# Expert layers as plain fp32 products from unsplit weights, seven whole-row gathers in flight, and a new order for the last tile

## The chip, the cores and the metric

The kernel runs on one core of one Trainium2 chip. The metric is the device time of one execution, in microseconds (us); lower is better. 0.3% of it, 2.4 us, is about what a measurement of this kernel can tell from no change.

## What is computed

Three residual blocks over x, 32 batches of 32 tokens with 512 features (1024 tokens):

```
x = x + cross_attention(layernorm(x), ctx, ctx, mask)      # 16 heads, 257 keys per batch
x = x + self_attention(layernorm(x))                       # 16 heads, rms-normed q and k
x = x + ffn(layernorm(x))

def ffn(x):
    x_mixed = k0 * x[s-1] + k1 * x[s] + k2 * x[s+1]        # along the tokens of a batch
    scores  = tanh(x_mixed @ Wo1 + bo1) @ Wo2 + bo2        # 9 scores for each token
    p       = argmax(scores)                               # one expert of 9
    y       = (x_mixed @ W1[p] + b1[p]) @ W2[p] + b2[p]    # 512 -> 128 -> 512, no nonlinearity
    return layernorm(x + y) * gamma + beta
```

The reference computes all nine experts and picks one; the kernel computes only the chosen one.

## The kernel before, in words

The kernel is written engine by engine, with semaphores and an order written out by hand. `T` is 1024 tokens, `P` is 128, so there are `NT` = 8 token tiles; `D` is 512, `CT` = 4 is the number of 128-wide chunks of a row, `E` is 9.

Cross attention comes first and is not touched, apart from where its weight tile `W_both` is allocated. Most products of both attentions are made as three products of split operands: every fp32 operand is cut into a high part, rounded to the reduced format `fp32r`, and the rest, and `three` (L92 to L96) issues high by high, low by high, high by low. `W_both` holds the high and low parts of five weights.

Self attention (`self_attention_and_experts`, L769) goes over the eight tiles in a software pipeline: iteration `it` projects q, k, v of tile `it - 1`, computes scores of tile `it - 2` and the output projection of tile `it - 3`. The last iterations are written out by hand, and with them the first part of the experts:

- `z3_make` writes the third layernorm of a tile, `z3_transposes` turns it, `mix_parts` (ScalarE) and `mix` (GpSimd) make the mixed rows, transposed, in `O_T`. For the last tile `mix_end` shares this between ScalarE, VectorE and GpSimd.
- `gate`, `tanh`, `gate_scores`, `choose` pick an expert for each token, in four groups of tiles (0 to 3, 4 and 5, 6, 7).
- `positions` (TensorE), `find_places` and `mark_places` (VectorE) and `map_tile` (TensorE, one tile at a time through the two buffers of `placed`) sort tokens by expert. `census`, `ranks`, `slot_lists` and `list_tokens` turn that into `NS` = 16 slots of up to 128 tokens of one expert, with the lists `to_slot` (which rows to fetch) and `from_slot` (where results go).
- `rows_transposes` and `rows_evac` turn the mixed rows back, and SyncE stores them to the DRAM tensor `rows`, whose rows hold 3 x 512 values: mixed row, `z3` row, and `x` plus `beta`. `m_rows` also stores the mixed rows alone in `rows_first`.
- The expert weights come in six loads of 768 KB into the two halves of `raw` and are split into `W_both`, as its attention weights fall out of use: `w_split` on ScalarE (L1698, one instruction a load) and on VectorE (L1976, three a load).

Then the sixteen slots run through all engines. GpSimd issues the gathers. Slots 0 and 1 fetch their mixed rows from `rows_first` into `z2` and `k_T` (`gather_first`), then whole rows (768 KB a slot) are fetched into a ring of seven buffers, `gather(k)`. Five are issued at once; slot 5 waits for the last weight split, and the rest go out one a slot:

```
for k in range(NS):
    make_root(k)
    if k:
        scatter(k - 1)
    if k + RING - 2 < NS:
        gather(k + RING - 2)
```

TensorE's order in the loop is `h_transpose(k - 1)`, `x_transposes(k + 1)`, `hidden(k)`, `outputs(k - 1)`. ScalarE's is `h_high(k - 1)`, `x_high(k + 1)`, `h_evac(k)`, `deviations(k - 2)`. VectorE makes the low parts (`x_low`, `h_low`) and does `residual`, `centre`, `finish`. `make_root(k)` on GpSimd needs the sum of squares of `deviations(k)`; `scatter(k)` writes 256 KB of finished rows to the output.

`idle` (L1477) issues products whose result nobody reads.

Of the kernel before, what the change touches and what calls it, by code (L numbers as in the profile page):

```python
# [60 lines left out]
def build(nc, io, out):  # L61
    ctx = ExitStack()
    with ctx:
# [14 lines left out]
        W_both = sb("W_both", [P, 2, 5, CT * D], F32R)  # L78
        W_hi, W_lo = W_both[:, 0], W_both[:, 1]
# [8 lines left out]
        cross_attention(nc, io, x_nat, ident, O_T, raw, W_hi, W_lo, bv, bo, o_b, o_first, w_in, whi, wlo, seen)  # L88
        self_attention_and_experts(nc, io, out, x_nat, ident, O_T, raw, W_both, bv, bo, o_b, first_pair, w_in, whi, wlo, seen)
# [678 lines left out]
def self_attention_and_experts(nc, io, out, x_nat, ident, O_T, raw, W_both, bv, bo, o_b, first_pair, w_in, whi, wlo, seen):  # L768
# [7 lines left out]
    with ExitStack() as ctx:  # L776
# [12 lines left out]
        e_both = W_both[:, :, :, :].rearrange("p a i n -> p a (i n)")  # L789
        w_hi, w_lo = ([W[:, i, :].rearrange("p (c n) -> p c n", c=CT) for i in range(5)] for W in (W_hi, W_lo))  # L790
        e_hi, e_lo = (W[:, :, :].rearrange("p i n -> p (i n)") for W in (W_hi, W_lo))
# [47 lines left out]
        GROUPS = ((0, 4), (4, 6), (6, 7), (7, 8))  # L839
        wo2, bo1, bo2 = sb("wo2", [P, E]), sb("bo1", [P, 1]), sb("bo2", [P, E])  # L840
# [10 lines left out]
        place, of_block = sb("place", [P, NT]), sb("of_block", [P, NT])  # L851
        place_i = sb("place_i", [P, NT], I32)
        placed = sb("placed", [P, 2, P + NB])
        junk9 = sb("junk9", [P, E])
# [9 lines left out]
        def th_of(g):  # L864
            at = (0, 0, 2 * P, 3 * P)[g]
            return bqkv[:, 1, at:at + (GROUPS[g][1] - GROUPS[g][0]) * P]

# [6 lines left out]
        rows_first = nc.dram_tensor("rows_first", (T, D), F32).ap()  # L874
# [5 lines left out]

        first_rows = (z2[:, :], k_T[:, :, :].rearrange("p c t -> p (c t)"))
# [10 lines left out]
        def x_halves(k):  # L892
            return (o_hi, o_lo) if k % 2 == 0 else o_first

        def h_rows(k):
            return z3s[:, k % 2 * 2 * P:(k % 2 + 1) * 2 * P]

        def h_halves(k):
            return z2_hi[:, k % 2, :], z2_lo[:, k % 2, :]


        def split_parts(i):

            src, n = raw[:, i % 2, 0:3 * D], 3 * D
            dst = [W[:, i * n:(i + 1) * n] for W in (e_hi, e_lo)]
            if i >= 3:
                return (src, *dst)
            return (src.rearrange("p (c e m) -> p c e m", c=CT, e=3),
                    *(w.rearrange("p (e c m) -> p c e m", c=CT, e=3) for w in dst))


        lists = (pw[0], pt[0], pw[0], pt[0])
        found = pw[0]
# [5 lines left out]
        def rows_bank(u):  # L919
            return pa[:, u % 2, :] if u else pw[1][:, :]  # L920
# [4 lines left out]
        def h_bank(k):  # L925
            return (pw[0][:, 0:2 * P], pa[:, 0, 0:2 * P])[k % 2]
# [4 lines left out]
        def y_bank(k):  # L931
# [4 lines left out]
        (w_hi_made, w_lo_made, mix_made, g_done, th_made, gs_done, choice_made, step3, pos_done, placed_made, map_done,  # L936
         counted, found_pe, found_dve, rowsT_done, rows_out) = (
            sem("x_" + n) for n in (
                "w_hi_made w_lo_made mix_made g_done th_made gs_done choice_made step3 pos_done placed_made map_done "
                "counted found_pe found_dve rowsT_done rows_out").split())  # L940
        (xT_done, xhi_made, xlo_made, h_done, h_out, hT_done, hhi_made, hlo_made, y_done, mean_made, squares_made,
         root_made, fin, last_mixed) = (
            sem("s_" + n) for n in (
                "xT_done xhi_made xlo_made h_done h_out hT_done hhi_made hlo_made y_done mean_made squares_made "
                "root_made fin last_mixed").split())
        x_first = [sem(f"x_first{i}") for i in range(2)]
# [40 lines left out]
        def _(eng):  # L987
# [1236 lines left out]
```

## Time and profile before

| | |
|---|---|
| median of 3 runs | 803.71 us (803.34 to 805.87) |
| the profiled execution, its own time | 801.18 us |
| its span, first to last instruction | 799.5 us |
| TensorE busy | 734.1 us (92%) |
| VectorE, ScalarE, GpSimd busy | 399.6, 345.4, 205.1 us |
| mean granted TensorE clock | 0.95 of full speed |
| HBM read, written | 47.45 MB, 12.58 MB |

The profile is of one execution. Its busy shares are an average over stages. The attentions take about the first 640 us, and there TensorE stands still little. The last 160 us look different: TensorE's share falls to 5 to 8 tenths, its granted clock falls with it, and the DMA engines are busy for 3 to 5 tenths. The change lies in these last 160 us, so it is read by stretches of time, by the timelines of TensorE and GpSimd there, and by the chain of waits.

### The profile page before, as it was taken

Reading aid. Unit: us, or ns where it says so; the run is one execution under the profiler, and the core shown is the slowest. Engines: PE = TensorE matmul, PEld = TensorE weight load, DVE = VectorE, ACT = ScalarE, POOL = GpSimd, SP = SyncE. Lnnn points to the kernel's source line nnn. Section 1 sums busy time; section 2 is a strip of 40 time slices with the busy share of each in tenths; the row PEclk is TensorE's granted clock in tenths of the full one; section 3 lists DMA queues with packets and bytes.
Section 4 is the critical chain, followed back from the end, with each engine's and each line's share of the span. In section 5 each row is a group of like instructions: output and inputs, shape, how many; then the busy total and the mean of one; then the engine's idle time right before and its main releaser. Section 6 shows DMA issues by size and latency. Waiting matters only on the chain. (4 is left out here: it accounts for less than half of the span.)

```text
span 799.5 us, 20785 instructions
## 1 busy us (share of the span) xinstructions
PE 734.1 (92%) x8232; PEld 582.1 (73%) x8232; DVE 399.6 (50%) x1045; ACT 345.4 (43%) x733; POOL 205.1 (26%) x299
## 2 busy tenths in 40 slices
PE   4999999999999999999999999899998986877773
PEld 3777778777877887787778777678777775666652
DVE  5544434343443244343424456657777767334555
ACT  3445444444444354444444454335445743222332
POOL 0001000010010010000100202776687642314455
PEclk9999999999999999999999999999999978577787
DMA  8211111011011101110120124300001135544540
GB/s 325 66 53 55 53 55 30 25 52 52 0 52 52 52 0 52 52 34 19 52 52 2 51 104 121 96 15 15 27 27 43 54 121 211 179 176 147 161 169 25
DMA packets 18871, 58.61 MB, mean 73 GB/s; under 512 B 6258, under 2 KB 6514, under 8 KB 15878
## 3 DMA queue, kind: packets, MB, share of 16 engines
q1 hardware_dynamic: 15078, 42.74, 15.8%
q0 software_dynamic: 3744, 15.21, 5.4%
q8 instruction: 32, 0.52, 0.3%
q14 instruction: 17, 0.14, 0.1%
HBM read 47.45 MB, written 12.58 MB: 75 GB/s over the span
## 5 line engine op out<-in xcount | busy, mean ns | idle before, releaser
L94 PE MATMUL pj<-W_both 128*128 128x512 f32 x544 | 222.4, 409 | 10.1 <-DVE W_both L593 10.1
L96 PE MATMUL pj<-W_both 128*128 128x512 f32 x544 | 213.8, 393 | 0.0
L95 PE MATMUL pj<-W_both 128*128 128x512 f32 x544 | 213.0, 392 | 0.0
L94 PEld LDWEIGHTS pj<-W_both 128*128 128x128 f32 x544 | 102.8, 189 | 43.8 <-issue 24.0
L96 PEld LDWEIGHTS pj<-W_both 128*128 128x128 f32 x544 | 102.8, 189 | 23.0
L95 PEld LDWEIGHTS pj<-W_both 128*128 128x128 f32 x544 | 103.1, 190 | 19.2
L234 POOL COPY q_b<-Q_T 128x128 f32 (+1 forms) x32 | 9.3, 292 | 416.9 <-PE tp L357 349.2
L491 ACT ACTIVATE K<-pj,bk 128x512 f32<-128x512 f32 x64 | 44.2, 690 | 136.9 <-PE pj L96 136.9
L652 DVE CUSTOM_DVE_ANT_0 m_flat<-sc,mask 128x257 f32<-128x257 f32 x64 | 24.7, 424 | 116.2 <-PE tp L357 94.9
L506 ACT ACTIVATE p_flat<-m_flat,nmax 128x257 f32<-128x257 f32 x128 | 63.8, 501 | 25.5 <-DVE nmax L652 25.4
L498 ACT ACTIVATE V<-pj 128x512 f32<-128x512 f32 x64 | 38.2, 597 | 73.1 <-PE pj L96 72.3
L593 DVE TENSOR_TENSOR W_both<-raw,W_both 128x2048 fp32r<-128x2048 f32 (+1 forms) x20 | 43.7, 2185 | 30.8 <-ACT W_both L450 30.8
L673 DVE COPY P_T<-tp 128x512 f32<-128x512 f32 x32 | 22.1, 691 | 66.6 <-PE tp L369 66.6
L1092 POOL TENSOR_TENSOR rms<-ms_eps,power 128x16 f32<-128x16 f32 x16 | 46.9, 2931 | 3.3 <-POOL ms_eps L1089 3.3
L661 DVE TENSOR_SCALAR p_flat<-p_flat,rinv 128x257 f32<-128x257 f32 x128 | 42.0, 391 | 1.1
L94 PE MATMUL pw<-W_both,z_hi 128*128 128x512 f32 x92 | 38.0, 413 | 1.0 <-DVE z_lo L1948 1.0
L450 ACT ACTIVATE W_both<-raw 128x2048 fp32r<-128x2048 f32 (+1 forms) x20 | 36.4, 1821 | 2.6 <-DMA raw<-wk_dram 2.6
L95 PE MATMUL pw<-W_both,z_lo 128*128 128x512 f32 x92 | 36.6, 397 | 0.0
L96 PE MATMUL pw<-W_both,z_hi 128*128 128x512 f32 x92 | 36.3, 395 | 0.0
L369 PE MATMUL tp<-ident,p_flat 128*128 128x128 f32 x256 | 33.1, 272 | 0.7 <-DVE P_T L673 0.7
L369 PEld LDWEIGHTS tp<-ident,p_flat 128*128 128x128 f32 x256 | 29.8, 140 | 4.8 <-issue 0.8
L684 DVE TENSOR_TENSOR O_T<-po,otail 128x128 f32 (+1 forms) x16 | 4.7, 292 | 43.4 <-PE po L389 43.3
(359 smaller groups left out, 1261.4 us busy)
## 6 DMA issues: line engine op xcount, KB each, us to landing
raw<-ctx_dram SPq DMA_DIRECT2D x15, 1024.0 KB, 4.7
raw<-w_dram SPq DMA_DIRECT2D x6, 768.0 KB, 4.5
raw<-w_dram SPq DMA_DIRECT2D x4, 1024.0 KB, 4.8
x_nat<-x_dram SPq DMA_DIRECT2D x2, 1024.0 KB, 12.5
rows<-z3s SPq DMA_DIRECT2D x8, 256.0 KB, 2.0
rows<-x_nat SPq DMA_DIRECT2D x8, 256.0 KB, 2.2
rows_first<-xm SPq DMA_DIRECT2D x8, 256.0 KB, 2.2
rows<-xm SPq DMA_DIRECT2D x8, 256.0 KB, 2.4
```

Of the source, the lines that this page charges most:

```text
L94: eng.matmul(out, a_hi, b_hi, start=first, stop=False)
L95: eng.matmul(out, a_lo, b_hi, start=False, stop=False)
L96: return eng.matmul(out, a_hi, b_lo, start=False, stop=last)
L369: mm = eng.transpose(tp[:, k, g * P:(g + 1) * P], probs[:, j, g, k * P:(k + 1) * P], ident[:, :])
L450: return eng.activation(dst, src, ACT.Copy)
L491: eng.activation(K[:, g, :, 0:SM], pj[g % 2][:, :].rearrange("p (j n) -> p j n", j=2), ACT.Identity, bias=bk[:, g:g + 1]).then_inc(k_out, 1)
L498: eng.activation(V[:, t, :], pj[t % 2][:, :], ACT.Copy).then_inc(v_out, 1)
L506: eng.activation(probs[:, j, g, :], masked[:, j, g, :], ACT.Exp, bias=nmax[:, j, g:g + 1], scale=-1.0, accum_out=psum_[:, j, g:g + 1]).the ...
L593: return eng.tensor_tensor(dst, src, hi.bitcast(F32), ALU.subtract)
L652: eng.tensor_tensor_reduce(masked[:, j, g, :], sc[g][:, 0:SK], mask[:, :], -1.0, BIG, ALU.add, ALU.min, nmax[:, j, g:g + 1]).then_inc(mask ...
L661: eng.tensor_scalar(probs[:, j, g, :], probs[:, j, g, :], rinv[:, j, g:g + 1], None, ALU.mult).then_inc(probs_made, 1)
L1092: eng.tensor_tensor(rms[:, heads], ms_eps[:, heads], power[:, heads], ALU.pow).then_inc(rms_made[i], 1)
```

## The change

It has four parts.

1. **Weights.** `experts`, plain fp32, takes the memory of `W_both` once a part of that is free. Layer one is in its first half (`w1_all`), layer two in its second (`w2_all`). SyncE loads straight into it, twelve DMAs: for layer one nine of 256 KB in pieces of 128 values, for layer two three of 768 KB. All `w_split` are gone, and with them gather 5's wait for the last split.
2. **Products.** `hidden` is a bias product and four fp32 products of 128 x 128, `outputs` a bias product and one fp32 product of 128 x 512; `h_transpose` is one transpose. ScalarE makes one copy where it made a high part (`xT_evac`, `hT_evac`), and `x_low`, `h_low` on VectorE are gone.
3. **Gathers.** `rows_first` and its eight stores are gone, as are `gather_first` and its two fetches. Seven gathers of whole rows are issued at once, then gather `k + 6` behind `scatter(k - 1)`.
4. **The last tile's order.** `map_tile` becomes `map_tiles` over three groups (`PLACED`: tiles 0 to 3, 4 and 5, 6 and 7), with marks for whole groups, `row_marks` and `block_marks`; `find_places` works on a group at once. `weighted_sum(NT + 1)` stands ahead of `gate_scores(1)`, `positions(0)` and the first `rows_transposes`; the four `idle` products between the last steps are gone, and the ten after them are four fp32 products.

```
-        W_both = sb("W_both", [P, 2, 5, CT * D], F32R)
+        with ExitStack() as attention:
+            W_both = sb("W_both", [P, 2, 5, CT * D], F32R, attention)
...
+        experts = sb("experts", [P, 2, 5, CT * D])
...
             def load(i):
-                need(eng, w_lo_made, 3 * (i - 1))
-                eng.dma_start(raw[:, i % 2, 0:3 * D], io["w1" if i < 3 else "w2"][i % 3]).then_inc(exw_in, 16)
-                eng.wait_ge(exw_in, 16 * (i + 1))
+                n = 3 * D
+                for j in range(3):
+                    eng.dma_start(w1_all[:, i * n + j * D:i * n + (j + 1) * D].rearrange("p (c m) -> p c m", c=CT),
+                                  io["w1"][i].rearrange("p (c e m) -> p c e m", c=CT, e=3)[:, :, j, :]).then_inc(exw_in, 16)
+                eng.dma_start(w2_all[:, i * n:(i + 1) * n], io["w2"][i]).then_inc(exw_in, 16)
...
             def m_rows(u):
                 eng.wait_ge(rows_out, u + 1)
-                eng.dma_start(rows_first[u * P:(u + 1) * P, :], mixed_rows(u)).then_inc(rows_in, 16)
                 eng.dma_start(at_rows(u, 0), mixed_rows(u)).then_inc(rows_in, 16)
...
             def gather(k):
-                if k < RING:
-                    if k == 5:
-                        eng.wait_ge(w_lo_made, 3 * 6)
-                else:
-                    eng.wait_ge(fin, k - RING + 1)
+                need(eng, fin, k - RING + 1)
...
-            for k in range(2):
-                gather_first(k)
-            for k in range(RING - 2):
+            for k in range(RING):
                 gather(k)
             for k in range(NS):
                 make_root(k)
                 if k:
                     scatter(k - 1)
-                if k + RING - 2 < NS:
-                    gather(k + RING - 2)
+                    if k + RING - 1 < NS:
+                        gather(k + RING - 1)
...
             def hidden(k):
-                out = h_bank(k).rearrange("p (i t) -> p i t", i=2)
                 for c in range(CT):
-                    for x in x_halves(k):
-                        eng.matmul(out, x[:, c, :], e_both[:, :, bass.ds(w_at + c * P, P)],
-                                   start=c == 0 and x is x_halves(k)[0], stop=False)
+                    mm = eng.matmul(h_bank(k), x_T(k)[:, c * P:(c + 1) * P], w1_all[:, bass.ds(w_at + c * P, P)],
+                                    start=False, stop=c == CT - 1)
...
             def outputs(k, w_at):
-                three(eng, y_bank(k), *h_halves(k), e_hi[:, w], e_lo[:, w], False, True).then_inc(y_done, 1)
+                eng.matmul(y_bank(k), h_T(k), w2_all[:, bass.ds(w_at, D)], start=False, stop=True).then_inc(y_done, 1)
```

**TensorE, one slot of the expert loop, before** (the end of slot 15's first layer, then slot 14's second; `first_pair` is the split rows, `z_hi` and `z_lo` the split hidden values, `z3s` the unsplit ones):

```order
L1504 MATMUL pa<-W_both,first_pair 128x256 x2
L1504 ISA
L1504 MATMUL pa<-W_both,first_pair 128x256 x2
L1506 MATMUL pa<-biases,of_slot 128x128
L1522 MATMUL pa<-biases,of_slot 128x512
L94 ISA
L94 MATMUL pa<-W_both,z_hi 128x512
L95 MATMUL pa<-W_both,z_lo 128x512
L96 ISA
L96 MATMUL pa<-W_both,z_hi 128x512
L1513 MATMUL pa<-ident,z3s 128x128 x2
```

and now, where the bias product of the first layer stands just ahead of these rows:

```order
L1476 ISA
L1476 MATMUL pa<-experts,e_T 128x128
L1476 ISA
L1476 MATMUL pa<-experts,e_T 128x128
L1476 ISA
L1476 MATMUL pa<-experts,e_T 128x128
L1476 ISA
L1476 MATMUL pa<-experts,e_T 128x128
L1489 MATMUL pa<-biases,of_slot 128x512
L1490 ISA
L1490 MATMUL pa<-experts,z3s 128x512
L1484 MATMUL pa<-ident,z3s 128x128
```

Eight products over 256 columns for each slot become four over 128, three over 512 become one, and two products that turn the hidden values become one transpose.

**TensorE, from the last tile's output projection to the lists, before** (`pa<-placed` is `map_tile`, `pa<-ident,O_T` is `rows_transposes`, `pa<-W_both` alone is `idle`):

```order
L1441 MATMUL pa<-placed 72x128
L1432 MATMUL pt<-choice,above 128x9
L1433 MATMUL pt<-chosen,ones 128x9
L1441 MATMUL pa<-placed 72x128
L1459 MATMUL pw<-ones,in_all 72x1
L1477 MATMUL pa<-W_both 128x512 x2
L1464 MATMUL pw<-used,above 72x1
L1477 MATMUL pa<-W_both 128x512 x2
L1441 MATMUL pa<-placed 72x128
L1470 MATMUL pw<-listed,tokens_T 128x16
```

and now:

```order
L1423 MATMUL pa<-sq_v,qk_qT 72x128 x2
L1412 MATMUL pw<-choice,above 128x18
L1413 MATMUL pw<-chosen,ones 128x18
L1439 MATMUL pw<-ones,in_all 72x1
L1433 MATMUL pa<-ident,O_T 128x128 x4
L1444 MATMUL pw<-used,above 72x1
L1433 MATMUL pa<-ident,O_T 128x128 x4
L1423 MATMUL pa<-sq_v,qk_qT 72x128 x2
L1450 MATMUL pw<-listed,tokens_T 128x16
```

The last two turns of rows stand where the idle products stood, and one group of two map products ends the list instead of single ones.

**GpSimd, the gathers, before:**

```order
L1198 DMA z<-rows_first,to_slot 128x512
L1198 DMA k_T<-rows_first,to_slot 128x512
L1207 DMA sq_v<-rows,to_slot 128x1536
L1207 DMA qk_qT<-rows,to_slot 128x1536
L1207 DMA xm<-rows,to_slot 128x1536
L1207 DMA O_T<-rows,to_slot 128x1536 x2
L1213 TENSOR_SCALAR root_in<-squares 128x1
L1214 TENSOR_TENSOR root<-root_in,power 128x1
L1207 DMA raw<-rows,to_slot 128x1536
```

and now:

```order
L1189 DMA sq_v<-rows,to_slot 128x1536
L1189 DMA qk_qT<-rows,to_slot 128x1536
L1189 DMA xm<-rows,to_slot 128x1536
L1189 DMA O_T<-rows,to_slot 128x1536 x2
L1189 DMA raw<-rows,to_slot 128x1536 x2
L1195 TENSOR_SCALAR root_in<-squares 128x1
L1196 TENSOR_TENSOR root<-root_in,power 128x1
L1195 TENSOR_SCALAR root_in<-squares 128x1
L1196 TENSOR_TENSOR root<-root_in,power 128x1
L1202 DMA out_dram<-xm,from_slot 1024x512
L1189 DMA sq_v<-rows,to_slot 128x1536
```

Gathers of slots 5 and 6 moved from behind the first roots to the opening burst; slot 7's is the first that a root holds back, root 1.

## Rows read from the trace of the kernel before

**Rows 1.** Stretches of 20 us: busy us (instructions) by engine, clock, DMA share, GB/s.

```profile
660.00:680.00 20.00, 13.51 (x77) 11.80 (x78) 13.71 (x45) 6.64 (x15) 3.92 (x7) 0.84 0.57 213
680.00:700.00 20.00, 16.40 (x66) 12.62 (x64) 7.06 (x27) 4.53 (x8) 7.00 (x7) 0.61 0.53 186
...
740.00:760.00 20.00, 15.79 (x70) 12.44 (x70) 10.97 (x24) 6.05 (x16) 8.87 (x13) 0.76 0.50 160
760.00:780.00 20.00, 15.10 (x76) 11.55 (x76) 11.13 (x26) 7.29 (x20) 10.56 (x15) 0.90 0.43 162
```

**Rows 2.** TensorE's timeline, last tile and first slots: start us, us, line, operation, count [idle before].

```profile
660.41 0.77 PE L94 MATMUL pw<-W_both,o_hi 128*128 128x512 f32 x1 [1.53 <-issue]
...
672.65 0.38 PE L1357 MATMUL pw<-ident,z3s 128*128 128x128 f32 x2
...
677.44 0.44 PE L1441 MATMUL pa<-placed 128*72 128x128 f32 x2 [3.83 <-DVE placed L2040]
...
686.86 1.20 PE L1477 MATMUL pa<-W_both 128*128 128x512 f32 x2
...
689.54 0.32 PE L1472 MATMUL pw<-listed,expert_of 72*41 72x16 f32 x2
...
694.67 1.12 PE L1488 MATMUL pt<-ident,z 128*128 128x128 f32 x4 [0.24 <-DMA z<-rows_first,to_slot]
...
703.67 1.11 PE L1488 MATMUL pt<-ident,xm 128*128 128x128 f32 x4 [3.65 <-DMA xm<-rows,to_slot]
```

**Rows 3.** GpSimd's timeline: first gathers, one slot's work late in the loop, last scatter.

```profile
691.01 1.35 POOL L1198 DMA_INDIRECT z<-rows_first,to_slot  x1 [13.71 <-DVE from_slot L2074]
...
766.51 0.42 POOL L1213 TENSOR_SCALAR root_in<-squares 128x1 f32<-128x1 f32 x1 [1.61 <-ACT e L1740]
...
769.19 1.00 POOL L1207 DMA_INDIRECT sq_v<-rows,to_slot  x1 [0.30 <-issue]
...
794.08 0.99 POOL L1220 DMA_INDIRECT out_dram<-xm,from_slot  x1 [0.30 <-issue]
```

**Rows 4.** Chain that ended last, one turn in the expert loop: start us, us, what.

```profile
768.69 0.67 PE pt L1488 x4
...
771.33 0.81 ACT e L1740 x2
...
774.65 4.58 DMA qk_qT<-rows,to_slot
779.27 0.66 PE pt L1488 x4
```

**Rows 5.** TensorE's timeline: two fp32 product groups (L1411), then one expert slot.

```profile
641.47 1.88 PE L1411 MATMUL pw<-O_T,raw 128*128 128x512 f32 x4
...
668.55 1.16 PE L1411 MATMUL pw<-O_T,raw 128*128 128x128 f32 x8 [1.74 <-DVE placed L2040]
...
774.88 1.21 PE L1504 MATMUL pa<-W_both,first_pair 128*128 x8 [0.23 <-issue]
...
776.18 0.44 PE L1522 MATMUL pa<-biases,of_slot 41*128 41x512 f32 x1
776.55 0.50 PE L94 MATMUL pa<-W_both,z_hi 128*128 x1
...
777.37 0.61 PE L1513 MATMUL pa<-ident,z3s 128*128 128x128 f32 x4
```

**Rows 6.** The same columns as rows 1, four us in the opening burst of gathers.

```profile
700.00:704.00 4.00, 0.35 (x3) 0.34 (x3) 0.29 (x1) 0.28 (x1) 0.00 (x0) 0.82 1.00 393
```

**Rows 7.** Instructions that touch `rows` from 685 us on: their DMA time.

```profile
DMA to landing us min/median/max: 4.6/5.3/8.5
```

**Rows 8.** Groups by line from 620 us on: count, busy us, mean ns, idle before.

```profile
L1976 DVE TENSOR_TENSOR W_both<-raw,W_both 128x512 fp32r<-128x512 f32 x18 | 11.3, 679 | 0.0
L1698 ACT ACTIVATE W_both<-raw 128x1536 fp32r<-128x1536 f32 x6 | 9.0, 1494 | 1.7 <-DMA raw<-w_dram 1.7
```

**Rows 9.** The page's DMA queue of SyncE: packets, MB, share of 16 engines.

```profile
q1 hardware_dynamic: 15078, 42.74, 15.8%
```

More of the change, by code:

```diff
@@ L890, in result, with x_T, h_T @@
             return xm[:, 1, k % 3 * D:(k % 3 + 1) * D]
-        def x_halves(k):
-            return (o_hi, o_lo) if k % 2 == 0 else o_first
+        def x_T(k):
+            return (e, e_T)[k % 2]
         def h_rows(k):
[L896 to L909, printed above, removed]
+            return z3s[:, k % 2 * P:(k % 2 + 1) * P]
+        def h_T(k):
+            return z3s[:, (2 + k % 2) * P:(3 + k % 2) * P]
         lists = (pw[0], pt[0], pw[0], pt[0])
+        places = (pw[0], pt[0], pw[0])
         found = pw[0]
@@ L1031, in _ @@
                     x_rows(u - 1)
+            eng.wait_ge(wo_done, NT)
+            load(0)
+            z_rows(5)
+            eng.wait_ge(qkv_done, 3 * NT - 2)
+            load(1)
+            eng.wait_ge(qkv_done, 3 * NT - 1)
             load(2)
[L1033 to L1034 removed]
             x_rows(4)
             x_rows(5)
[L1037 removed]
+            eng.wait_ge(x1b_made, NT)
+            eng.dma_start(gamma, row_on_all(io["gamma"])).then_inc(exw_in, 16)
             z_rows(6)
+            m_rows(0)
+            z_rows(7)
+            for u in range(1, 5):
+                m_rows(u)
             x_rows(6)
[L1040 to L1048 removed]
             x_rows(7)
[L1050 to L1051 removed]
+            for u in range(5, NT):
+                m_rows(u)
         @block.gpsimd
@@ L1424, in gate_scores, with positions @@
                 mm.then_inc(gs_done, 1)
-            def positions(g):
-                a, b = GROUPS[g]
-                to = lists[g][:, 0:(b - a) * E]
-                eng.wait_ge(choice_made, g + 1)
-                need(eng, counted, b - 1)
+            def positions(q):
+                a, b = PLACED[q]
+                to = places[q][:, 0:(b - a) * E]
+                eng.wait_ge(choice_made, q + 1 if q < 2 else len(GROUPS))
+                eng.wait_ge(counted, b - 1)
                 eng.matmul(to, above[:, :], choice[:, a:b, :].rearrange("p t e -> p (t e)"), start=True, stop=False)
@@ L1655, in mix_parts @@
                 eng.wait_ge(mix_made, u + 1)
-                for a, dst in ((1, O_T), (0, o_b), (2, mixed)):
+                for a in some:
+                    dst = (o_b, O_T, mixed)[a]
                     for c in range(CT):
@@ L1739, in deviations @@
                 need(eng, squares_made, k)
-                eng.activation(e[:, :], slot(k, 1), ACT.Square, bias=mean[:, k:k + 1],
+                eng.activation(mixed[:, :, :].rearrange("p c t -> p (c t)"), slot(k, 1), ACT.Square, bias=mean[:, k:k + 1],
                                accum_out=squares[:, k:k + 1]).then_inc(squares_made, 1)
@@ L1795, in _ @@
                     deviations(k - 2)
-            h_high(NS - 1)
+            hT_evac(NS - 1)
             deviations(NS - 2)
@@ L2021, in choose, with find_places @@
                                              in1=before, op0=ALU.is_equal, op1=ALU.add).then_inc(counted, 1)
-            def find_places(g):
-                a, b = GROUPS[g]
-                eng.wait_ge(choice_made, g + 1)
-                eng.wait_ge(pos_done, g + 1)
-                for t in range(a, b):
-                    ch3.link(eng.tensor_tensor_reduce(junk9[:, :], lists[g][:, (t - a) * E:(t - a + 1) * E], choice[:, t, :], 1.0, 0.0,
-                                                      ALU.mult, ALU.add, place[:, t:t + 1]))
+            def find_places(q):
+                a, b = PLACED[q]
+                n = b - a
+                got = places[q][:, 0:n * E].rearrange("p (t e) -> p t e", t=n)
+                eng.wait_ge(choice_made, q + 1 if q < 2 else len(GROUPS))
+                eng.wait_ge(pos_done, q + 1)
+                eng.wait_ge(counted, b)
+                ch3.link(eng.tensor_tensor(key[:, 0:n, :], got, choice[:, a:b, :], ALU.mult))
+                eng.tensor_reduce(place[:, a:b], key[:, 0:n, :], AX.X, ALU.add).then_inc(places_made, 1)
+                eng.wait_ge(places_made, q + 1)
                 ch3.link(eng.tensor_copy(place_i[:, a:b], place[:, a:b]))
```

304 lines of the change are left out of this document (102 added, 202 removed).

## The prediction

> **What bounds the kernel now.** I read the stretches of time first, then TensorE's timeline, the chain of waits, and GpSimd's timeline. Up to 640 us TensorE is nearly always busy, and the change leaves that part alone. From 660 us on it is busy for 13.5 to 16.4 us of every 20, at a granted clock between 0.61 and 0.90 of full speed [rows 1]. Two stages lie there. Up to the lists of rows to fetch, ready at 689.9 us, TensorE hands small results to VectorE and waits for them, once for 3.83 us [rows 2]. Then come the sixteen slots: first gather at 691.0 us, last scatter at 794.1 us, end of the span at 799.5 us [rows 3]. So the expert loop is 108.5 us.
>
> In the loop no engine is full. The chain of waits shows a ring: the turn of slot 13's rows at 768.69, the deviations at 771.33, the gather at 774.65 with 4.58 us to landing, the turn of slot 15's rows at 779.27 [rows 4]. That is 10.6 us for two slots, 5.3 a slot, with the clock up; it is longer where the clock is down. The gather of slot k + 5 goes out behind root k. Root k needs `deviations(k)`, which ScalarE has behind `h_evac(k + 2)`, and that needs slot k + 3's rows, which TensorE turns ahead of `hidden(k + 2)`. So a gather is issued only two slots ahead of its use, though the ring of buffers has seven places. Latency sets the pace.
>
> **The loop, step by step.** *Lead.* Now gather k + 6 stands behind root k, three slots ahead. The same chain, 10.6 us, spread over three slots, is 3.5 us a slot.
>
> *GpSimd* then comes first. Root, scatter and gather of one slot run from 766.51 to 770.19 us [rows 3]: 3.7 us, with the hand-over 3.8 us. Nothing of it is removed. I take 3.8.
>
> *TensorE.* A slot at full clock now: turn of rows 0.45 (four transposes, shown as 0.67 with the tail [rows 4]), first layer with bias 1.30, second 1.19, turn of hidden values 0.5 (spacing of the starts, and the last row's 0.61 less its tail [rows 5]); with hand-overs 3.9. After the change: an fp32 product over 512 columns takes 0.9 us (1.88 us for two), one over 128 takes 0.25 to 0.29 (1.16 us for four, less the tail) [rows 5]. So first layer 1.0 + 0.15 for the bias, second 0.35 + 0.9, one transpose 0.11, rows 0.45: 2.9 us. At half clock it is some 5.7 us. Even here TensorE gains 1.0 us a slot, and its gaps, 0.9 us in 3.8, are shorter than those of the stretch whose clock was 0.90 [rows 1].
>
> The first layer gains although the array's work stays the same. In the old form eight products took 1.21 us [rows 5]. The Trainium skill, "FP8 and Floating Point Precision", section "TensorE Precision Notes", says that true FP32 takes four passes through the array. By it alone the first layer is 4 x 128 x 4 columns against 8 x 256, no gain, and the second 512 x 4 against 3 x 512, a loss of 512 columns, 0.2 us at full clock; the sum would then owe nothing to the products. The 0.9 us for 512 columns agrees with four passes, so I book only the 1.0 us above, most of it from the turn of the hidden values and the first layer's shorter issue.
>
> *VectorE* loses the two low parts of each slot and *ScalarE* has the same count of copies; both have room below 3.8 us, so I book nothing but their part in the tail.
>
> *Start.* The opening gathers run at 393 GB/s with the DMA engines full [rows 6]; a gather of 786,432 B then takes 2.0 us, and 5.3 us from issue to landing [rows 7]. Slot 0's rows are there 5.4 us after the first issue; before, the small fetch let TensorE start after 3.7 (694.67 less 691.01) [rows 2, 3]. That is 1.7 us lost. But slot 2 lands at 9.4 where five big gathers behind two small ones had it at 12.7 (the turn at 703.67, after a wait of 3.65 us [rows 2]), and slot 6 at 17.6. Counting from the first issue: first layer of slot 0 ends at 10.0, each slot takes 2.9, slot 3's first layer ends at 18.0, so root 1 can start at 19.2, and gather 7 starts 2.7 later, at 21.9 (766.51 to 769.19 in rows 3). Eight more gathers at 3.8 put gather 15 at 52.3, landing at 57.6. Before, slot 15's rows were turned at 88.3 (779.27 less 691.01).
>
> *Tail.* From there to the end was 20.2 us [rows 4] (799.5 less 779.27). Two slots of TensorE at 1.0 less and an `x_low` and two `h_low` gone from the path (0.7 us for 512 columns, the kind of subtraction in rows 8, less for 128) make it 17; GpSimd's remaining roots and scatters fit in. So the loop is 57.6 + 17 = 74.6 us against 108.5: 34 less. I expect one fallback of the clock, where slot 7 is first waited for, worth 3 us: **31 us**.
>
> **The stage before the loop.** The splits (11.3 us VectorE, 9.0 us ScalarE [rows 8]) mostly lay beside TensorE's work; I price them at 0 by themselves, for TensorE was the cover, and it stays. The order is worth more. (a) The output projection of the last tile started at 660.41 after a wait of 1.53, since `weighted_sum` stood behind a gate score, positions and a turn of rows; now those fill the wait, 2 to 3 us. (b) Its `z3` rows were turned at 672.65, 7 us after the projection's end; fewer steps stand ahead of that on TensorE and ScalarE, 1 to 2 us. (c) The wait of 3.83 us at 677.44 for VectorE's marks goes, but the last choice has six small operations and three larger ones for two tiles at once behind it: 1 to 3 us. (d) Two pairs of `idle` products, 1.1 us a pair, stood ahead of the last map product: 1 to 2 us [rows 2]. Against that, the last mixed rows are now turned just ahead of the lists, so their store and not the lists may release the first gather: 0 to 1 us lost. Steps (a) to (d) overlap. Bounds 0 and 11; I take **7 us**, near the middle, since each stands on a wait seen in rows 2.
>
> *Loads.* SyncE's queue now has nine DMAs in 512 B pieces, 4608 of them. Nothing in the trace is such a load. The queue's 15078 packets took 15.8% of 16 engines' span [rows 9], 134 ns a packet of 2.8 KB on average; at that price 288 pieces an engine take 39 us, at a price by bytes 6 us. I estimate that they are issued between 620 and 635 us, among the stores of tiles 4 to 6, and so end between 641 and 674 us, before the idle products ask for them near 683. I price them at 0. If the cover were gone, each us late is a us late. The Trainium skill, "DMA: Bandwidth & Descriptors", section "Specifications", gives 512 B as the least size for line rate; these pieces are just that, so by it the price is the lower one. The eight stores to `rows_first` were off the path: 0.
>
> **Sum.** 7 + 31 = 38 us off the profiled execution's 801.2 (1.7 around the span of 799.5) gives 763. The median of the runs is 2.5 higher, 803.7; against it the forecast is **766 us**.
>
> **Rivals.** (A) *The clock stays mixed.* If TensorE runs at 0.76 of its clock through the loop, as from 740 to 760 [rows 1], a slot takes 4.3 us, over GpSimd's 3.8, from the start: 10 + 14 x 4.3 + 18 = 88, a gain of 20, with the first stage 777. For it: every long wait for a gather was followed by half clock. Against it: the gaps get shorter than those at 0.90 [rows 1]. (B) *The third slot of lead is lost*, because a gather behind a scatter and two others lands later than 5.3 us (8.5 was the most [rows 7]), or the stage pace falls back to two slots a turn: 21.9 + 8 x 4.8 + 5.3 + 17 = 83, with the first stage between 0 and 7: 771 to 778. (C) *Half clock eats the gain:* all slots at 5.7 us: 10 + 14 x 5.7 + 23 = 113, 4 more than now, less 7: 801, no change or nearly. (D) *Slower:* fp32 products at half clock with their weight loads uncovered, eight loads a slot at 0.1 us each. A slot is then 6.5 us, the loop 10 + 91 + 25 = 126, and with nothing gained before it the time is 821; with the 7, 814. It decides once a slot passes 5.9 us, the present mean (88.3 us for 15 slots). Against it: the fp32 products in rows 5 show no such gaps.
>
> **How the numbers follow.** Forecast 60%, A 20, B 13, C 2, D 5. Forecast range: 11 + 36 at best, 757; at worst 0 + 25, 779. A and B end inside or near it; I put the range at **755 to 784 us**. Differences of 0.3%, 2.4 us, are what a measurement can tell: faster 0.93, same 0.02, slower 0.05.
>
> **What would show it.** Right: first gather near 684 us of the span; gathers in the loop 3.7 to 4.0 us apart and starting right behind GpSimd's scatters; x turns waiting under 1 us; TensorE near 2.9 us a slot at a clock of 0.9; loop near 77 us. Step wrong if: the chain still alternates gather, turn, deviations, root over two slots (B); clock under 0.8 from 700 us on (A); GpSimd idle before its first gather ended by a DMA of `rows` and not by the lists; loads landing after 680 us. A loop above 95 us would make the whole prediction wrong.

## The result, and the profile after

The changed kernel takes 772.11 us (median of 4 runs, 770.54 to 775.83); the kernel before, on the same chip, 803.53 us. The ratio is 0.961, 95% interval 0.957 to 0.965. The forecast was 766 us, the range 755 to 784. The profiled execution took 770.54 us, its span is 768.8 us; the prediction's sum for it was 763. Two slow executions in the experiments are left out of all numbers below: one of `e_best_again` at 773.82 us, and one of `e_best` at 1376.8 us, in which TensorE's products took some 1.7 times their usual time, at a granted clock of 1.00 in the records.

The page's head, its busy times, its row of the granted clock, and the loads of the experts' weights:

```profile
span 768.8 us, 20525 instructions
...
PE 722.8 (94%) x8158; PEld 561.6 (73%) x8158; DVE 373.9 (49%) x978; ACT 335.6 (44%) x727; POOL 203.2 (26%) x297
...
PEclk9999999999999999999999999999999998767998
...
experts<-w_dram SPq DMA_DIRECT2D x9, 256.0 KB, 4.3
experts<-w_dram SPq DMA_DIRECT2D x3, 768.0 KB, 6.7
```

The stretches that answer to [rows 1], with the same columns:

```profile
680.00:700.00 20.00, 16.32 (x55) 10.37 (x55) 1.49 (x9) 3.50 (x8) 6.88 (x7) 0.67 0.76 296
700.00:720.00 20.00, 19.36 (x87) 12.25 (x86) 11.03 (x24) 9.26 (x25) 9.82 (x14) 0.91 0.33 107
720.00:740.00 20.00, 16.71 (x84) 10.51 (x82) 11.26 (x25) 8.29 (x23) 14.08 (x20) 1.00 0.72 240
740.00:760.00 20.00, 16.64 (x71) 9.38 (x71) 13.41 (x30) 9.69 (x27) 14.03 (x20) 1.00 0.34 122
```

From 720 to 760 us the granted clock is full, where it was 0.76 between 740 and 760 before [rows 1]. Between 680 and 700 us, where the loop starts, it is 0.67 (0.61 before). TensorE is now busy for 16.3 to 19.4 us of every 20 from 680 to 760 us. The loads land in 4.3 and 6.7 us, long before they are needed.

TensorE's timeline, last tile and first slots, answers to [rows 2]:

```profile
659.22 0.77 PE L96 MATMUL pw<-W_both,o_hi 128*128 128x512 f32 x1
...
668.29 0.44 PE L1337 MATMUL pw<-ident,z3s 128*128 128x128 f32 x2 [0.59 <-ACT z3s L1579]
...
682.81 0.32 PE L1452 MATMUL pw<-listed,expert_of 72*41 72x16 f32 x2
...
689.55 0.66 PE L1465 MATMUL pt<-ident,sq_v 128*128 128x128 f32 x4 [1.03 <-DMA sq_v<-rows,to_slot]
691.88 0.66 PE L1465 MATMUL pt<-ident,qk_qT 128*128 128x128 f32 x4 [1.67 <-DMA qk_qT<-rows,to_slot]
```

The lists are ready 6.7 us earlier (682.81 against 689.54). GpSimd's timeline, which answers to [rows 3]:

```profile
684.28 1.25 POOL L1189 DMA_INDIRECT sq_v<-rows,to_slot  x1 [11.22 <-DVE from_slot L2011]
...
708.88 0.20 POOL L1195 TENSOR_SCALAR root_in<-squares 128x1 f32<-128x1 f32 x1 [2.52 <-ACT mixed L1694]
...
711.45 1.18 POOL L1189 DMA_INDIRECT sq_v<-rows,to_slot  x1 [0.30 <-issue]
712.69 0.19 POOL L1195 TENSOR_SCALAR root_in<-squares 128x1 f32<-128x1 f32 x1
712.97 0.56 POOL L1196 TENSOR_TENSOR root<-root_in,power 128x1 f32<-128x1 f32 x1
713.74 1.55 POOL L1202 DMA_INDIRECT out_dram<-xm,from_slot  x1 [0.21 <-issue]
715.60 0.98 POOL L1189 DMA_INDIRECT qk_qT<-rows,to_slot  x1 [0.30 <-issue]
...
744.41 0.99 POOL L1189 DMA_INDIRECT qk_qT<-rows,to_slot  x1 [0.30 <-issue]
```

The first gather stands at 684.28 (691.01 before), and the loop from there to the span's end is 84.5 us (108.5 before): 6.7 and 24.0 us gained. Gather 7 is the one at 711.45, gather 15 the one at 744.41: eight steps of 4.12 us on average. From 711.45 to 715.60 GpSimd goes from gather to root to scatter to gather without waiting for another engine, and the chain that ended last runs through it alone from 708.88 to 726.84 us, in steps of 3.50 to 4.15 us. Further on it changes:

```profile
725.45 1.09 POOL out_dram L1202
...
726.84 7.56 DMA O_T<-rows,to_slot
...
734.45 0.67 PE pt L1465 x4
```

Here a gather takes 7.56 us to land, and TensorE, ScalarE and GpSimd wait for it. From issue to landing a gather takes 6.2 us in the median here (5.3 before), and up to 11.1. The loop has two bounds close together, GpSimd's row and the ring of gathers.

### The profile page after: what moved, and what is told of

Its sections match the earlier page's. It is cut to its first block and busy times, and to the rows that moved or that the text cites. A ratio compares the mean times of both kernels' runs of the same rounds, so it can differ in the third digit from the quotient of the medians.

```text
span 768.8 us, 20525 instructions
## 1 busy us (share of the span) xinstructions
PE 722.8 (94%) x8158; PEld 561.6 (73%) x8158; DVE 373.9 (49%) x978; ACT 335.6 (44%) x727; POOL 203.2 (26%) x297
## 5 line engine op out<-in xcount | busy, mean ns | idle before, releaser
L96 PEld LDWEIGHTS pj<-W_both 128*128 128x128 f32 x544 | 102.6, 189 | 43.3 <-issue 23.6
```

The lines of the kernel that those rows point to most:

```text
L96: eng.matmul(out, a_hi, b_hi, start=first, stop=False)
```

## The experiments

All kernels were timed beside the kernel before, whose median lay between 802.1 and 803.6 us. "Loop" is always first gather to the span's end in the profiled execution, "pitch" an eighth of the time from gather 7 to gather 15. Between executions of the changed forms the first gather moves by about 2 us for no reason of the edit (682.7 to 685.1 us in seven kernels whose code ahead of it does the same or nearly so), so a stage effect under 2 us isn't read from one trace. Much of that is there early: an output projection of TensorE near 619 us, ahead of every edit that is compared below, starts anywhere from 618.23 to 620.94 us.

### The lead, alone and taken away

`b_lead3` is the kernel before with the longer lead alone; `e_lead2` is the changed kernel with the lead of before.

```
b_lead3:                                  e_lead2:
-            for k in range(RING - 2):    -            for k in range(RING):
+            for k in range(RING):        +            for k in range(RING - 1):
...
-                if k + RING - 2 < NS:    -                    if k + RING - 1 < NS:
-                    gather(k + RING - 2) -                        gather(k + RING - 1)
+                    if k + RING - 1 < NS:     +               if k + RING - 2 < NS:
+                        gather(k + RING - 1)  +                   gather(k + RING - 2)
```

> The changed kernel with one gather less in flight: six at the start, then gather k + 5 behind root k, two slots ahead as in the kernel before. All products stay fp32. Theory 'lead' (the distance between a gather's issue and its use set the pace of the loop): gather, turn, deviations, root again close over two slots, about 5.1 us a slot for ten gathers instead of 4.1 for nine, so some 13 us slower than the changed kernel: about 785 us. Rival 'products' (the shorter work on TensorE made the loop faster): within 3 us of the changed kernel, 770 to 775 us.

> The kernel before with only the new order of the gathers: all seven at the start (the two last behind the last weight split, as their buffers demand), then gather k + 6 behind root k. Split products, early rows and the old order of the last tile stay. Theory 'lead': about 18 us faster than before, near 785 us, with 4.2 to 4.5 us a slot. Rival 'products': within 5 us of the kernel before, since TensorE's 3.9 us a slot at full clock and 7 at half clock stay.

Measured: `e_lead2` 798.28 us, ratio 0.993 (0.990 to 0.996), loop 112.8 us. `b_lead3` 779.94 us, ratio 0.971 (0.968 to 0.974), loop 85.5 us. So

| loop, us | products of before | new products, no early rows |
|---|---|---|
| gather k + 5 behind root k | 108.5 | 112.8 |
| gather k + 6 behind root k | 85.5 | 84.5 |

The lead alone brings 23.6 of the 31.4 us, and once the lead is there the new products, together with the loss of the early rows, change the loop by 1 us. With the old lead the loop is even 4 us longer than before. The right column differs from the left in both things, so neither difference is the products' alone. TensorE in `e_lead2`, the turns of rows of five slots in a row, with their waits:

```profile
725.31 1.06 PE L1465 MATMUL pt<-ident,sq_v 128*128 128x128 f32 x4
...
731.30 0.66 PE L1465 MATMUL pt<-ident,qk_qT 128*128 128x128 f32 x4 [1.72 <-DMA qk_qT<-rows,to_slot]
...
737.64 1.12 PE L1465 MATMUL pt<-ident,xm 128*128 128x128 f32 x4 [2.61 <-DMA xm<-rows,to_slot]
...
743.89 1.06 PE L1465 MATMUL pt<-ident,O_T 128*128 128x128 f32 x4
...
750.09 1.00 PE L1465 MATMUL pt<-ident,O_T 128*128 128x128 f32 x4
```

Here is the ring of [rows 4] again, at 6.2 us a slot. And the granted clock falls with the waits: 0.76, 0.76, 0.67 and 0.76 in the four stretches from 700 to 780 us. That was not in my 785 us for this run: a wait for a gather is paid twice, once as a wait and once as slower products after it. In `b_lead3` the clock is 1.00 from 720 to 760.

The slot from 743.89 to 750.09 lies wholly at half clock (0.50 in each stretch of it) and has no wait in it: 6.20 us. The kernel before has such a slot too, here from first layer to first layer, and it takes 5.94 us:

```profile
704.44 2.07 PE L1504 MATMUL pa<-W_both,first_pair 128*128 x8
...
710.38 2.06 PE L1504 MATMUL pw<-W_both,o_pair 128*128 x8
```

So at half clock the new form is the slower one, by 0.26 us a slot.

What the products are worth by themselves, at full clock. `b_lead3`, one slot in the old form:

```profile
712.12 0.60 PE L1488 MATMUL pt<-ident,O_T 128*128 128x128 f32 x4
712.48 1.16 PE L1504 MATMUL pw<-W_both,o_pair 128*128 x8
713.57 0.32 PE L1506 MATMUL pw<-biases,of_slot 41*128 41x128 f32 x1
713.73 0.44 PE L1522 MATMUL pa<-biases,of_slot 41*128 41x512 f32 x1
714.10 0.50 PE L94 MATMUL pa<-W_both,z_hi 128*128 x1
...
714.92 0.61 PE L1513 MATMUL pw<-ident,z3s 128*128 128x128 f32 x4
715.36 0.60 PE L1488 MATMUL pt<-ident,O_T 128*128 128x128 f32 x4
```

The changed kernel, one slot:

```profile
705.84 0.60 PE L1465 MATMUL pt<-ident,O_T 128*128 128x128 f32 x4
706.37 0.32 PE L1474 MATMUL pa<-biases,of_slot 41*128 41x128 f32 x1
706.62 1.16 PE L1476 MATMUL pa<-experts,e_T 128*128 x8
707.71 0.49 PE L1489 MATMUL pa<-biases,of_slot 41*128 41x512 f32 x1
708.13 1.12 PE L1490 MATMUL pa<-experts,z3s 128*128 x2
709.09 0.27 PE L1484 MATMUL pa<-ident,z3s 128*128 128x128 f32 x1
709.20 0.60 PE L1465 MATMUL pt<-ident,raw 128*128 128x128 f32 x4
```

3.24 us in the old form (715.36 less 712.12), 3.36 in the new (709.20 less 705.84). The first layer costs 1.09 in both, by the spacing of the starts; the second layer goes from 0.82 to 0.96, the hidden values' turn drops from 0.44 to 0.11, and the bias products cost 0.14 and the turn of the rows 0.17 more. The neighbouring slots without a wait agree within 0.02 us in both traces.

### The cold start

Why does the clock read 0.50 from 694 to 702 us, at the start of the loop? The changed kernel's four idle products end before the rows are there, and TensorE stands still for 1.03 us and, after the first turn, for 1.67 us; then the granted clock falls to half of full speed, 1.2 GHz. `e_warm` puts unread products into both gaps:

```
-            idle(4)
+            idle(5)
 
             x_transposes(0)
+            idle(2)
             x_transposes(1)
```

> The changed kernel with one more unread product ahead of the first turn of rows and two between the first and the second turn, where TensorE stood still for 1.03 and 1.67 us. Theory 'cold start' (these gaps lowered the clock from 693 to 703 us of the span, and slots 0 to 2 took 5 us instead of 3): the clock stays at full speed there, root 1 comes about 4.5 us earlier, and the whole is 4 to 5 us faster, near 768 us. Rival 'GpSimd sets the pace from root 1 on, and from the gathers' landing before': under 1.5 us gained. Second rival: the fall of the clock has nothing to do with the gaps, and the clock is half again from 693 us: 0, or 1 us slower where the extra products come late.

Measured: 767.23 us, ratio 0.956 (0.952 to 0.960), 4.9 us less than the changed kernel. Its stretch from 680 us:

```profile
680.00:700.00 20.00, 17.10 (x71) 9.72 (x72) 2.29 (x10) 4.21 (x10) 6.90 (x7) 0.91 0.77 296
```

The gaps are not gone but shorter, 0.71 and 1.19 us, and the clock is 1.00 in every 2 us from 686 to 706 us. Gather 7 goes out 24.0 us after the first, against 27.2, and the loop is 80.9 us against 84.5. So the cold start cost 3.6 us. The two medians alone would not settle it, as their intervals overlap; the clock and the loop do.

### The order of gather and scatter

`e_gather_first` issues gather k + 6 ahead of `scatter(k - 1)`.

```
                 if k:
-                    scatter(k - 1)
                     if k + RING - 1 < NS:
                         gather(k + RING - 1)
+                    scatter(k - 1)
```

> The changed kernel with gather k + 6 ahead of scatter k - 1 on GpSimd instead of behind it; both need the same finished slot. Theory 'landing' (slots wait for gathers that leave 1.4 us late): waits of the row turns for DMAs (0.2 to 1.3 us each in the changed kernel) fall to near 0 and the whole is 2 to 4 us faster. Rival 'GpSimd is full': its 3.8 us a slot stay, gathers leave once, not each time, 1.4 us earlier: 1 to 1.5 us faster and not more.

Measured: 769.45 us, ratio 0.961 (0.956 to 0.966), loop 84.3 us against 84.5, pitch 4.24 against 4.12. The median is 2.7 us lower, but the ratio is that of the changed kernel and the loop is as long: no gain is shown. The gather went out 1.5 us nearer to its root, but it reuses the buffer of slot k - 1, which VectorE had not yet finished with:

```profile
720.62 1.03 POOL L1189 DMA_INDIRECT O_T<-rows,to_slot  x1 [1.25 <-DVE xm L2030]
```

The scatter stood there in a time that GpSimd had to wait anyway.

### What sets the pitch: GpSimd or the gathers

Three kernels on `e_warm`. `e_warm_root_twice` does the power of `make_root` twice. `e_warm_fold` takes one operation of GpSimd away: the mean's factor goes into gamma and the small epsilon is left out. `e_small_gather` fetches only two thirds of each row: it leaves out the x part, so the residual adds stale values.

```
e_warm_root_twice:
+                own.link(eng.tensor_tensor(root[:, one], root_in[:, one], power[:, 0:1], ALU.pow))
e_warm_fold:
-                own.link(eng.tensor_scalar(root_in[:, one], squares[:, one], 1.0 / D, LN_EPS, ALU.mult, ALU.add))
e_small_gather:
-                eng.indirect_dma_start(slots[k % RING], None, rows,
+                eng.indirect_dma_start(slots[k % RING][:, 0:2 * D], None, rows_two,
```

> e_warm with the power that makes each root computed twice, the second with the same result: 0.65 us more on GpSimd for each slot. Theory 'GpSimd sets the pace' (root, scatter and gather take 3.8 us a slot and TensorE only 3.4): the nine gathers that wait for roots move from 4.1 to about 4.6 us apart, and the whole is 5 to 7 us slower, 772 to 774 us. Rival 'TensorE or VectorE set the pace': under 2 us slower. A ring of waits over three slots would take 0.65 / 3 us a slot: 2 to 3 us slower.

> e_warm with one GpSimd operation less for each slot (0.28 us): the root is taken of the sum of squares itself, the square root of 512 goes into gamma once, and the epsilon of the last layernorm (1e-5 beside a variance near 1) is left out. Theory 'GpSimd sets the pace': 2 to 3 us faster than e_warm, 764 to 765 us. Rival 'ring over three slots': 1 us. Rival 'TensorE': 0.

> e_warm with gathers of two thirds of each row (512 KB instead of 768 KB); the x part of the rows is not fetched, so the last addition adds stale values. Theory 'GpSimd sets the pace': the opening burst is quicker, which TensorE cannot use in full (slot 1 is there 0.6 us earlier, slot 2 by 1.3 us), later slots keep 3.8 to 4.1 us; 1 to 2.5 us faster than e_warm. Rival 'bytes set the pace' (the DMA engines were busy 65 to 72% in the loop, and some gathers took 7.6 us to land): waits of the row turns vanish and it is 5 us faster or more, 762 us or less.

| | time, us | ratio (95%) | loop | pitch | GpSimd's waits in the eight steps |
|---|---|---|---|---|---|
| `e_warm` | 767.23 | 0.956 (0.952 to 0.960) | 80.9 | 4.07 | 2.6 |
| `e_warm_root_twice` | 772.41 | 0.964 (0.958 to 0.971) | 86.6 | 4.44 | 0 |
| `e_warm_fold` | 763.31 | 0.952 (0.946 to 0.958) | 78.5 | 3.84 | 4.5 |
| `e_small_gather` | 762.97 | 0.951 (0.946 to 0.957) | 76.1 | 3.72 | 0.5 |

Both count. 0.6 to 1.0 us more on GpSimd cost 0.37 us a slot and took all its waits away; 0.28 us less gave 0.23 and left it waiting longer; a third less to fetch gave 0.35. With small gathers GpSimd hardly waits, and its steps are 3.5 us where its scatter and its gather each take their usual 1.0 to 1.1 us (up to 4.2 where one takes longer):

```profile
711.86 0.98 POOL L1190 DMA_INDIRECT qk_qT<-rows_two,to_slot  x1 [0.30 <-issue]
...
715.34 0.99 POOL L1190 DMA_INDIRECT xm<-rows_two,to_slot  x1 [0.30 <-issue]
```

### The loads and a gap in TensorE

The loads of the experts' weights were priced at 0. But where they run, TensorE stands still with no releaser named, which it did for 0.19 us before:

```profile
638.16 0.59 PE L1391 MATMUL pw<-O_T,raw 128*128 128x512 f32 x1 [2.60 <-issue]
```

`e_warm_late` is `e_warm` with the second and third third of the loads moved behind a later store of `z3` rows:

```
             load(0)
             z_rows(5)
-            eng.wait_ge(qkv_done, 3 * NT - 2)
-            load(1)
-            eng.wait_ge(qkv_done, 3 * NT - 1)
-            load(2)
             x_rows(4)
...
             z_rows(6)
+            eng.wait_ge(qkv_done, 3 * NT - 1)
+            load(1)
+            load(2)
             m_rows(0)
```

> e_warm with the second and third block of expert weights loaded later: behind z row store 6 (near 650 us of the span) instead of near 627 to 632 us. Theory 'code fetch' (TensorE's unexplained gap of 2.60 us at 635.5 to 638.2 us, where the kernel before had 0.19 us, comes because its instructions are fetched by DMA engines that are busy with these loads): the gap goes, the first gather leaves 2 to 2.5 us earlier, near 681.5 us, and the whole is 2 us faster than e_warm, near 765 us. Rival 'the gap belongs to the code's place, not to the loads': no gain. Second rival: the later loads collide with another fetch of code or with the store of rows, and the gap moves.

Measured: 762.80 us, ratio 0.952 (0.947 to 0.958), 4.4 us less than `e_warm`; first gather at 679.80 us against 683.45 (0.6 of that was there before the loads), loop 81.0 against 80.9. The same place on TensorE now has no gap:

```profile
635.01 0.73 PE L96 MATMUL pw<-W_both,o_hi 128*128 128x512 f32 x1
```

That the loads make the gap is shown, since it goes when they are moved: it is 2.54 to 3.37 us in the seven traces with all loads early and 0.26 us or nothing in the four with two thirds of them late. In the changed kernel the clock reads 0.50 from 640 to 642 us, behind the gap, and 1.00 there in `e_warm_late`; that may be part of the 3.65 us, which are more than the gap. That it is TensorE's own code arriving late behind them, through DMA engines that were 0.92 busy, is only argued, from the missing releaser; the page does list a queue for instructions.

### What made the first stage shorter

Two kernels on `e_warm_late`. `e_junk_splits` puts copies of the size of five of the six removed splits back (data that nobody reads). `e_sum_later` puts `weighted_sum(NT + 1)` back to its old place.

```
e_junk_splits, ScalarE five times and VectorE five times at places of the splits:
+                eng.activation(raw[:, 0, 0:3 * D], raw[:, 0, 0:3 * D], ACT.Copy).then_inc(act_junk, 1)
...
+                for j in range(3):
+                    part = raw[:, 1, j * D:(j + 1) * D]
+                    eng.tensor_tensor(part, part, part, ALU.subtract).then_inc(dve_junk, 1)
e_sum_later:
-            weighted_sum(NT + 1)
             gate_scores(1)
             positions(0)
+            weighted_sum(NT + 1)
             out_proj(NT + 2)
```

> The changed kernel with the longer warm-up and the late loads (as in the run before it that had both, 762.8 us, first gather at 679.8), and with copies of the size of the removed splits put back where they stood: five copies of 128x1536 on ScalarE (about 1.5 us each) and fifteen operations of 128x512 on VectorE (about 0.68 us each), on data that nobody reads. The result is unchanged. Theory A, the order of the last tile's work gave the 6.7 us of the stage and the splits hardly anything: first gather 1.5 us later at most (681.3 or less), time 762 to 765. Theory B, the splits held up ScalarE and VectorE on the path that sets the first gather: first gather 4 us or more later (683.8 or more), time 767 or more.

> The same kernel as base (longer warm-up, late loads; 762.8 us, first gather at 679.8), with one thing of the old order put back: the weighted sum of the last tile but one stands behind the gate scores and positions again instead of ahead of them. Theory A, this place in the order made the wait of 3.8 us before the transposes of the rows: first gather 2 to 4 us later, time 765 to 767. Theory B, the wait came from what other engines had to do, so that the place on TensorE matters little: within 1 us, 762 to 764.

`e_junk_splits`: 767.28 us, ratio 0.957 (0.952 to 0.963), first gather at 682.16: 2.4 us later in the trace, 4.5 in the medians, whose intervals overlap. By the first gather it falls between the two theories, by the time into the second. And 1.5 of the 2.4 us were there before the first copy, which starts at 621.62; this is the same wait of TensorE in `e_warm_late` and in `e_junk_splits`:

```profile
618.23 0.50 PE L96 MATMUL pw<-W_both,o_hi 128*128 128x512 f32 x1 [1.18 <-DVE o_lo L1836]
...
619.72 0.50 PE L96 MATMUL pw<-W_both,o_hi 128*128 128x512 f32 x1 [1.19 <-DVE o_lo L1850]
```

So the size stays open between 0.9 and 4.5 us. What the trace does show is that the copies delay VectorE's small results, and TensorE with them:

```profile
665.12 0.37 PE L1412 MATMUL pt<-choice,above 128*128 128x18 f32 x2 [1.71 <-DVE chosen L1965]
...
670.01 2.28 PE L1391 MATMUL pt<-O_T,raw 128*128 128x128 f32 x8 [1.66 <-DVE O_T L2004]
```

In `e_warm_late` the first wait is 0.61 us and the second isn't there; in the other kernels with the new order they are at most 0.61 and 0.77 us.

`e_sum_later`: 764.88 us, ratio 0.954 (0.947 to 0.960), first gather at 683.68. TensorE was already 2.1 us behind at 645.87 us, ahead of the edit, so of the 3.9 us only 1.8 can be the edit's; the medians differ by 2.1. Before the last output projection, where [rows 2] show a wait of 1.53 us and the changed kernel has none, there is again one of 1.42:

```profile
659.37 0.80 PE L96 MATMUL pw<-W_both,o_hi 128*128 128x512 f32 x1 [1.42 <-DVE o_lo L1836]
```

The difference of the two medians is within what the intervals allow, so what is shown is this wait of 1.4 us; the rest of the 2 us is not.

### One more operation off GpSimd

`e_best` is `e_warm_late` with `root_in` made on ScalarE.

```
-                own.link(eng.tensor_scalar(root_in[:, one], squares[:, one], 1.0 / D, LN_EPS, ALU.mult, ALU.add))
...
+                eng.wait_ge(sum_made, k + 1)
+                eng.activation(root_in[:, k:k + 1], squares[:, k:k + 1], ACT.Identity, bias=ln_eps[:, 0:1],
+                               scale=1.0 / D).then_inc(squares_made, 1)
```

> The same kernel as base (longer warm-up, late loads; 762.8 us, loop 81.0 us), with the operation that makes the mean square (one 128x1 multiply and add on GpSimd in each slot) moved to ScalarE, behind the sum of squares there. GpSimd loses about 0.28 us in each slot, ScalarE gains about 0.3 us of work and a hop. Theory A, GpSimd's own row of work sets the pace of slots 7 to 15: loop 1.5 to 3 us shorter, time 760 to 761.5. Theory B, the chain from ScalarE's sum to the gather sets it: the loop is as long or up to 1 us longer, time 762.5 to 764.

> The kernel of the run before, unchanged, once more: its profiled execution was one in which every product of TensorE took twice its time (1375 us), while the four others gave 759.0 to 760.0 us, so that its trace doesn't show the loop. Asked is where the 3 us against the 762.8 us of its base come from. Theory A, GpSimd's row of work sets the pace of slots 7 to 15: loop 78 to 79.5 us against 81.0, gathers 7 to 15 about 3.8 us apart. Theory B, the chain from ScalarE sets it and the 3 us lie ahead of the loop: loop 81 us or more, first gather ahead of 679.8. Time 759 to 761 by both.

Measured: 759.63 us, ratio 0.947 (0.942 to 0.952), and, run again, 762.08 us, 0.949 (0.946 to 0.953). In the second's trace the loop is 80.0 us against 81.0, the pitch 3.94 against 4.05, the first gather at 679.38. GpSimd lost the operation, and waits for the new one instead:

```profile
712.44 0.56 POOL L1196 TENSOR_TENSOR root<-root_in,power 128x1 f32<-128x1 f32 x1 [1.27 <-ACT root_in L1698]
```

Neither theory: 1 us, where GpSimd alone would have given 1.5 to 3. Against `e_warm_late` (762.80) it isn't told from no change. Both are 10 to 12 us faster than the changed kernel: 0.95 of before.

## Why the prediction was right, and which of its steps were wrong

The time lay in the range, on the side forecast, and for the reason given; it was 6.1 us above the forecast. By its steps:

- **Lead: right.** "Latency sets the pace" and the third slot of lead lifts it: 23 us of loop by `b_lead3`, 28 by taking it away in `e_lead2` (112.8 less 84.5).
- **GpSimd comes first: right for its own row, 0.3 us a slot short for the loop.** 3.8 us forecast, 4.12 measured; eight steps make 2.6 us (32.96 against 30.4). GpSimd's own row is 3.76 us on average, 3.50 to 4.29 in the steps without a wait. The rest is three waits of 1.54, 0.93 and 0.40 us; the two long ones are for ScalarE's sums, which wait for late gathers: 6.2 us to land in the median, 7.56 late in the loop, where I took 5.3, though 8.5 stood in [rows 7]. Rival B named this; it came as a part, not as a case.
- **TensorE's 1.0 us from the products: wrong.** I took the slot before as 3.9 us with hand-overs, the parts read from [rows 5] being 3.4, and set 2.9 without hand-overs against it. At full clock the old form takes 3.24 us and the new one 3.36. The first layer's eight products over 256 columns and four fp32 products over 128 both come to 1.09 us. The Trainium skill, "FP8 and Floating Point Precision", section "TensorE Precision Notes", states four passes through the array for true FP32; worked out as in the prediction, the first layer then gains nothing and the second loses. The trace agrees: 1.09 us and 1.09 us, and 0.82 against 0.96. I had the rule beside the sum and booked against it. It costs little at the end, as TensorE isn't the bound of the later slots; it is some 1.4 us of gather 7's delay.
- **Start: wrong in size.** The first turn came at 5.3 us after the first gather (forecast 5.4), the second at 7.6 (7.4). Then I had root 1 at 19.2 and gather 7 at 21.9; they came at 24.6 and 27.2. Of these 5.3 us, 3.2 are the half clock (`e_warm` has 24.0). The remaining 2.1 match 0.46 us more for each of three slots, 1.4 us, and 0.7 us that the sum itself dropped: three slots of 2.9 us after 10.0 end at 18.7, where it has 18.0. I had booked a fallback of the clock worth 3 us, but late, at slot 7; it came at slots 0 to 2, behind the two waits for the first gathers, which I had counted as time and not as a cost in clock.
- **Tail: 2.1 us short.** From gather 15 to the end 24.4 us, forecast 22.3.
- Sum of the loop: forecast 31, measured 24.0. The missing 7.0 us are 5.3 less the 3 booked, 2.6 and 2.1.
- **Stage before the loop: 7 forecast, 6.7 measured, partly by luck.** 1.4 of the 6.7 us were there near 619 us, ahead of the stage (618.73 against 620.12). And two errors work against each other. The splits, priced at 0, were worth something, between 0.9 and 4.5 us (`e_junk_splits`): TensorE was no cover for them, as it waited for the same engines. The loads, also priced at 0, cost 2.4 us (2.60 less 0.19) in a place where I only asked when they end, not what else the DMA engines serve meanwhile; their landing in 4.3 and 6.7 us was the lower of my two prices. Of (a) to (d), (a) is seen as 1.4 us in `e_sum_later`; (b) is seen as 4.4 us (668.29 against 672.65), of which 1.2 were there when the projection started (659.22 against 660.41); the wait of (c) is gone. Their shares apart were not tested.
- **Rivals.** A and C named a clock that stays low: in the loop it was low for 8 to 10 us and then full. A's 4.3 us a slot did not follow from its own terms, as 2.9 us at 0.76 of the clock are 3.8; it would have been GpSimd's pace. D, slower, did not come about with the lead, but `e_lead2` shows what it had right: the changed kernel without the lead has the longer loop, 112.8 against 108.5, at a clock of 0.67 to 0.76. A slot at half clock takes 6.20 us, between C's 5.7 and D's 6.5 and above the 5.9 from which D said it decides. How the 4.3 us divide between the fp32 products, 0.12 to 0.26 us a slot by the slots shown above, and the missing early rows was not taken apart.

## What to carry to other kernels

In a ring of gathers, count how many uses ahead each gather is issued, and test that alone first: here one more slot of lead was three quarters of the gain, and without it the rest of the change saved 5 us. Take the cost of an engine's work from a place where it waits for nothing and its clock is full, and compare both forms there. Before a loop that starts on a gather, shorten the gaps of TensorE up to and between its first turns with unread products; and put large loads where no engine depends on what else the DMA engines bring.

## What the runs showed of the hardware

- After gaps of 1.03 and 1.67 us on TensorE, the granted clock read 0.50 for about 8 us and came back while TensorE was busy without a break; with gaps of 0.71 and 1.19 us in the same places (`e_warm`) it stayed at 1.00.

```profile
694.00:696.00 2.00, 1.63 (x9) 1.29 (x7) 0.00 (x0) 0.56 (x2) 0.00 (x0) 0.50 0.99 415
...
704.00:706.00 2.00, 2.00 (x10) 1.11 (x9) 0.00 (x0) 0.98 (x3) 0.40 (x2) 1.00 0.00 0
```

- TensorE stood still for 2.60 us beside twelve loads, 4608 KB together, though it reads none of their data there; with eight of them later it did not.
- A slot of the new form takes 3.36 us at full clock and 6.20 at half, one of the old form 3.24 and 5.94: on TensorE the three products of split operands cost no more here than plain fp32.
- Of two gathers of 768 KB issued late in the loop, one took 7.56 us and the other 4.78 us to land.
